# Probabilities times values in the first attention: four key tiles at a time, at two points of a head

## The reference

```python
q = (v @ WQ).reshape(B, S, H, C)            # v: layernorm(h), 16 x 1024 x 64; 8 heads of 64
k = (v @ WK).reshape(B, S, H, C)
val = (v @ WV).reshape(B, S, H, C)
scores = jnp.einsum('bshc,bthc->bsth', q, k) * SCALE
A = jax.nn.softmax(scores, axis=2)          # over the 1024 keys t
u = jnp.einsum('bsth,bthc->bshc', A, val).reshape(B, S, H * C)
return u @ Wout + bout
```

## Time and profile before

| | |
|---|---|
| median of 3 runs | 5754.56 us (5752.11 to 5756.6) |
| profiled execution, own time | 5764.91 us |
| its span | 5763.2 us |
| mean granted TensorE clock | 0.910 of full speed |
| TensorE busy over the span | 5001.3 us (87%) |
| first attention, first to last `values` | 1062.7 to 3196.2 us |

### The profile page before, as it was taken

The page is one execution under the profiler, slowest core; times in us unless marked ns, Lnnn a source line. Parts: engine busy times, 40 slices in busy tenths (PEclk is TensorE's granted clock), DMA queues, the critical chain, the costliest instruction groups (busy, mean ns, idle before and its releaser), DMA issues. The chain is left out here.

```text
span 5763.2 us, 123600 instructions
## 1 busy us (share of the span) xinstructions
PE 5001.3 (87%) x42227; PEld 2282.0 (40%) x42227; DVE 3975.3 (69%) x7258; ACT 3151.1 (55%) x3356; POOL 2073.4 (36%) x1997
## 2 busy tenths in 40 slices
PE   2678878899999999999999599999999999997454
PEld 1334434333333333333333244444444444443223
DVE  2665665566666666666666488888888888887666
ACT  0222222466666666666666167777777777774111
POOL 1021222322322323223323455656556566563000
PEclk9787888899999999999999689999999999997555
DMA  1211110000000000000000000000000000000000
GB/s 28 73 44 29 44 44 15 1 2 2 1 2 2 2 2 1 2 1 2 1 2 1 1 2 3 2 3 2 3 3 2 3 2 3 3 2 2 11 7 11
DMA packets 43483, 52.85 MB, mean 9 GB/s; under 512 B 33124, under 2 KB 33255, under 8 KB 42856
## 3 DMA queue, kind: packets, MB, share of 16 engines
q1 hardware_dynamic: 39798, 43.81, 2.8%
q10 hardware_dynamic: 3058, 0.89, 0.1%
HBM read 39.68 MB, written 4.19 MB: 8 GB/s over the span
## 5 line engine op out<-in xcount | busy, mean ns | idle before, releaser
L1523 DVE TENSOR_REDUCE a_mp<-psum 128x1 f32<-128x512 f32 x2072 | 1321.4, 685 | 682.1 <-PE psum L1400 674.6
L2159 DVE TENSOR_REDUCE f_mp<-psum 128x1 f32<-128x512 f32 (+2 forms) x2614 | 1344.0, 574 | 232.3 <-PE psum L2007 180.8
L1957 ACT ACTIVATE f_prob<-psum,escale_f 128x1024 f32<-128x1024 f32 x1152 | 1242.6, 1112 | 276.6 <-PE psum L2075 147.7
L1372 ACT ACTIVATE a_prob<-psum,escale 128x1024 f32<-128x1024 f32 x1024 | 1087.9, 1111 | 522.2 <-PE psum L1449 521.9
L1457 PE MATMUL psum<-a_prob,a_v 128*64 128x512 f32 x4104 | 996.3, 606 | 0.0
L1997 PE MATMUL psum<-f_kf,f_qf 64*128 64x512 f16 (+3 forms) x3138 | 676.4, 332 | 51.4 <-DVE f_mp L2159 43.9
L1842 POOL TENSOR_SCALAR f_hi<-f_raw,part 128x512 f16<-128x512 f32 x330 | 516.7, 1566 | 471.6 <-ACT f_raw L1924 471.6
L2088 PE MATMUL psum<-f_prob,f_vh 128*32 128x512 f32 (+3 forms) x6144 | 614.7, 495 | 3.3
L1302 POOL TENSOR_TENSOR a_u<-a_og,a_inv 128x512 f32<-128x512 f32 x129 | 134.6, 1043 | 1150.7 <-DVE a_inv L1538 1150.7
L2067 PE MATMUL psum<-f_qf,f_kf 64*128 64x512 f16 (+3 forms) x3074 | 512.0, 329 | 28.3 <-issue 17.8
L1457 PEld LDWEIGHTS psum<-a_prob,a_v 128*64 128x64 f32 x4104 | 249.3, 136 | 512.5 <-issue 510.8
(11 more groups left out here) (399 smaller groups left out, 7473.8 us busy)
## 6 DMA issues: line engine op xcount, KB each, us to landing
l_idx<-in_itok_BS_dram SPq DMA_DIRECT2D x36, 512.0 KB, 5.7
l_idx<-in_itok_BS_dram SPq DMA_DIRECT2D x54, 256.0 KB, 6.7
l_idx<-in_x_dram SPq DMA_DIRECT2D x18, 256.0 KB, 3.5
a_qh<-a_rowT SPq DMA_DIRECT2D x258, 1.0 KB
out_dram<-h SPq DMA_DIRECT2D x16, 256.0 KB, 2.6
f_qf<-f_rowT SPq DMA_DIRECT2D x130, 4.0 KB, 1.8
wd<-in_L_ffn_Wd_dram ACTq DMA_DIRECT2D x1, 256.0 KB
wd<-in_L_ffn_Wd_dram SPq DMA_DIRECT2D x1, 256.0 KB
```

Of the source, the lines that this page charges most:

```text
L1372: act.activation(prob[:, part], k.psum[:, pair:pair + 2].rearrange("p b n -> p (b n)"), ACT.Exp, scale=k.escale[:]).then_inc(s.read, 1)
L1523: dve.tensor_reduce(mp[:, tg % 2, t + 4 * r, c:c + 1], bank_of(j + r), X, ALU.max)\
L1957: act.activation(prob[:, u % NPF], k.psum[:, pair:pair + 2], ACT.Exp, scale=k.escale_f[:])\
L2159: ins = dve.tensor_reduce(side[:, at:at + 1], bank_of(j + r)[:, col:col + nk], X, ALU.max)
```

## The change

The products of probabilities and values are issued for four key tiles at once, at slot 6 (tiles 0 to 3) and at slot 0 of the next head (tiles 4 to 7, due 8). Before, two tiles at once were issued at slots 2, 4, 6 and at slot 1 of the next head. The order inside the slots is new, and so are the places of the other items: `q` stands behind `exp` 0 (before: 1), `out` behind `exp` 5 (before: 3), and `x` behind `exp` 7 (before: 0). ScalarE copies the sum behind `exp` 0 (before: 1). It waits for a group of `values` by `part // 4`, and GpSimd clears four tiles of `prob` at the start in place of two. `row` stays in slot 5, where it now comes behind `S`.

```diff
-A_PARTS = ((0, 1), (2, 3), (4, 5), (6, 7))
+A_PARTS = ((0, 1, 2, 3), (4, 5, 6, 7))
 NAV = len(A_PARTS)
-A_VALUES_AT = (2, 4, 6, 9)
-A_ORDER = ('SM', 'VSM', 'SVM', 'S01', 'SMV', 'MS', 'SMV', 'MS')
+A_VALUES_AT = (6, 8)
+A_ORDER = ('0VS1', 'MS', 'MS', 'MS', '0S1', 'S01', 'SMV', 'MS')
 A_HEADS = {"M": (0, 1), "0": (0,), "1": (1,)}
-A_EXTRA = {0: (('x', 0),), 1: (('q', 2),), 3: (('out', -1),)}
-A_COPY_AT = 1
+A_EXTRA = {0: (('q', 2),), 5: (('out', -1),), 7: (('x', 0),)}
+A_COPY_AT = 0
...
-                pool.memset(prob[:, 6:8], 0.0).then_inc(s.clear, 1)
+                pool.memset(prob[:, 4:8], 0.0).then_inc(s.clear, 1)
...
-                            act.wait_ge(s.pv, n_pv(G - 1, part // 2))
+                            act.wait_ge(s.pv, n_pv(G - 1, part // 4))
```

## The result

The changed kernel takes 5853.9 us (median of 4 runs, 5852.7 to 5855.5) against 5755.6 for the kernel before on the same chip: 1.0172 times, 95% interval 1.0154 to 1.019, 98 us slower. The forecast was 5855. The profiled executions, 5855.5 and 5764.9 us by their own times, lie 90.6 us apart.

A forecast was written before the change was run, and what follows sets the result against it. TensorE was taken to bound the first attention before, ScalarE to set the pace between blocks after. +95 (heads), +4 (`x`) and +2 (clearing) gave +101 us, 5855 against the median; forecast range 5830 to 5885, 80% range 5770 to 5900.

The forecast's parts named there:

- The walk: One head followed item by item from the end of slot 0's block, ScalarE setting the pace between blocks: 17.07 us.
- The handover of 0.25: From the end of a tile's scores on TensorE to ScalarE's next exp: 0.25 us, ends 0.22 and 0.30.
- the 0.32 us that TensorE alone would gain: TensorE's own work in a head, without waits, falls from 16.33 to 16.01 us; over 128 heads -41 us.
- the tally: Sum of TensorE's own steps, entries and exits in a head after the change: 16.01 us.
- seams: Switches on TensorE between work in row halves and work over all rows: 1.30 us of the head before.
- rival 1: TensorE still sets the pace and the kernel gets faster, 16.01 us a head, 5720 us; chance 12%.
- VectorE "stays hidden by 0.9": Before slot 6's block, VectorE's reductions are done at 7.6 us, TensorE comes at 8.55: no cost.
- reductions of line 1523 that end TensorE's waits: Sign in the profile after that would show the forecast wrong: TensorE waiting for VectorE's reductions; no size given.
- The bound of +0.37 a head: Lower bound of the loss, ScalarE between the blocks without any handover: 16.70 us a head.
- fewer waits and the longer block behind the loop's jump: nothing: Small term at the loop's jump back: no change in time, since the same work runs there.
- Rival 4, the clock: New waits let TensorE's clock fall; one block in ten at the lower level adds 88 us, 5943; chance 5%.
- TensorE busy near 94%: Sign in the profile after that would confirm the forecast: TensorE's busy share of the stage near 94%.

The follow-up runs named there:

- half_both_after: The changed kernel with both cuts: ScalarE takes exp of half of the queries, VectorE reduces half of the columns of each maxima product; 5731.9 us.
- the control: The kernel before with the same two cuts, exp of half of the queries and maxima over half of the columns; 5735.0 us.

## Why the prediction was right, and where it was not

**Right: the time and its main sum.** The walk gave 17.07 us a head, and it is 17.09. Point by point, with time 0 at the end of the block in slot 0 (2014.87): exp 1 at 1.65 (1.70 predicted), `out` at 5.86 (5.95), the block of slot 6 at 8.88 (8.86; `out` at 2003.64 and the block at 2006.66 are 3.02 apart), the second block 4.77 behind it (4.77). The handover of 0.25 was a little long: five exponentials run at 1.02, not at the 1.035 of the round of 2.07. `out` and `row` were taken a little short: 1.19 us to the maxima (2020.73 to 2021.92, 2003.64 to 2004.83) in place of 0.84 + 0.25. The two errors cancel. Three waits for ScalarE a head are there, and the two stretches of ScalarE idle (3.38 and 2.61 us). With VectorE relieved and ScalarE at its full length the head is 17.08, so the cause that the walk names gives this time by itself.

**The total was closer than its parts.** That 5855 met 5853.9 is in part luck. The prediction added 101 us; the medians lie 98 us apart, the profiled executions 90.6 and the stages 87.5 (below). A gain of 15 us at the loop's jumps was not foreseen, and the kernel before's profiled execution stood 9 us above its median where the changed kernel's stood 2.

**Wrong: the 0.32 us that TensorE alone would gain.** 16.01 us was forecast and 16.21 measured with both cuts. Half of this 0.20 is `out` with `row`, 1.19 in place of 1.09 as above. The other half stands between `q` and `out`: 20 steps, 4.30 us, take 4.40 (2011.38 to 2015.78), where the row halves still run apart a little. (The text on record for `half_both_after` reached 16.2 another way: it counted `out` as 1.04, to the start of `row`, though the entry into `row` was already in the tally.) And 16.33, from which the tally was taken, held 0.09 of waits for VectorE. The prediction put 1.30 us down to seams, but those that it lists add up to 1.17 (four entries 0.40, two exits 0.32, into and out of `row` 0.30, to `q` and back 0.15); the other 0.13 it counted as saved. So the gain of the seams is 0.03 us a head beside the control, and rival 1 would have had nothing to give even if ScalarE had kept up.

**Wrong: VectorE "stays hidden by 0.9".** This step failed, and the sign of it that the prediction named, reductions of line 1523 that end TensorE's waits, is in the rows (283 of them). I asked only when the last maximum before the block gets its bank. TensorE issues in order, so the maxima of slots 2 and 3 already stand in front of the scores behind them. Halving exp leaves 16.96 us. The bound of +0.37 a head, "ScalarE without any handover", could thus not have been reached; with exp halved VectorE still held the head at +0.63. The prediction named one of two causes of nearly equal size, and its time was right since the slower of the two sets it.

**Wrong: "fewer waits and the longer block behind the loop's jump: nothing".** In the kernel before, the first jump back costs what the earlier trace rows show, an idle time and a block at the lower clock. The idle time is there at all seven jumps inside the stage (1.67 to 2.21 us), but the slow block only at the first and the fourth (3.16 and 3.29 us). The second jump has the longest idle time, and its block runs at full rate:

```profile
1596.71 0.39 PE L1449 MATMUL psum<-a_qh,a_xh 64*128 64x512 f16 x2 [2.21 <-issue]
...
1597.68 1.94 PE L1457 MATMUL psum<-a_prob,a_v 128*64 128x512 f32 x8
```

In the changed kernel:

```profile
1329.80 3.65 PE L1457 MATMUL psum<-a_prob,a_v 128*64 128x512 f32 x16
...
1335.03 3.65 PE L1457 MATMUL psum<-a_prob,a_v 128*64 128x512 f32 x16
```

The blocks on both sides of the jump are 5.23 us apart in place of 4.77, and both run at full rate (3.65 us), as they do at all seven jumps. From `row` to `row` the seven heads with a jump take 0.81 to 1.11 us over a plain one (the first from 1327.35 to 1345.37), 6.7 in all. In the kernel before they take 2.32 to 2.85 over it where the clock stays, and 4.43 (1320.85 to 1341.61) and 4.36 where it falls, 21.7 in all. (In both kernels 0.47 us of it lies ahead of the jump, where a maximum waits for the copy of the row.) So the jumps give back 15 us. The windows agree: from 1330 to 1350 us the granted clock was 0.94 before and is 1.00 now. That the long block ahead of the jump covers it is my reading; no run took it away alone.

**The small terms.** A head with `x` takes 1.50 us more than a plain one (slot-6 block 3237.28 to 3255.87). In the kernel before it takes 17.59 us from `row` to `row` (3139.26 to 3156.85), 1.25 or 1.26 more. So `x` costs 0.25 in each of 16 heads, the +4 of the prediction. `q` does wait for GpSimd's split as foreseen, 0.34 us at one head:

```profile
3243.18 3.65 PE L1457 MATMUL psum<-a_prob,a_v 128*64 128x512 f32 x16
...
3244.73 2.13 POOL L1289 TENSOR_TENSOR a_xl<-a_xraw,a_xh 128x1024 f16<-128x1024 f32 x1 [0.18 <-POOL a_xh L1287]
...
3247.01 0.41 PE L1424 MATMUL psum<-a_xh,wa 128*64 128x512 f16 x2 [0.17 <-POOL a_xl L1289]
```

Clearing two more tiles took 1.7 us (3.51 in place of the 1.81 of the earlier trace rows). The fourth head of each iteration takes 0.24 us more than a plain one now (17.33 us, 8 times, +2), and the cause of that stays open. Together: plain heads 127 x 0.76 = +96.5, `x` +4, jumps -15, these +2, sum some +87.5. By the slot-6 blocks of the first and the last head, 1069.72 and 3273.43, the stage grew from 2116.2 to 2203.7 us, +87.5. Of the rest, 3 us lie outside these heads (90.6 between the profiled executions), and 8 us are the difference between single executions and medians.

**The rivals.** Rival 4, the clock, did not come: 1.00 granted from 1066 to 3290 us. By the section of the Trainium skill cited there ("TensorE: Matmul & The Clock Gate") frequent short idles can make it go to and fro; this trace does not show it with waits of up to 0.5 us several times a head, and it even lost the two falls behind a jump. "TensorE busy near 94%" was the wrong sign to look for, as the windows above show.

## What to carry to other kernels

A bound engine that issues in order is also the pump of the others: a long burst on it lets their queues run dry, and behind the burst they need their time per item again. Check each of them on its own against the slots between two bursts, item by item with its buffers, and not only up to the last item; two may stand behind each other, so that relieving one shows little (18 and 9 us here, against 122 for both). Before seams are grouped away, ask what the small blocks hide, since here they covered VectorE's reductions, ScalarE's exponentials and a row's transfer.

## What was not expected of the hardware

A jump back of the loop cost a head 2.3 to 4.4 us where 1.7 us blocks stood around it and 0.8 to 1.1 us where 3.4 us blocks did. TensorE's clock fell only in the first case, at two jumps of seven, behind idle times of 2.14 and 2.02 us; behind 2.21 and 2.10 us at two others it stayed. `out`, the same 16 matmuls, takes 0.84 us to the next product in row halves and 1.04 to the row, which goes over all rows; an entry into other work over all rows took 0.10 of that. And the profile's busy share in 500 us of the stage rose, from 99.2% to 99.8%, while TensorE did 4% fewer matmuls.
